# Attention weighing with 64-column products, row sums from ScalarE's accumulator, halves added on VectorE

## What is computed

```python
query, key, value = layernorm(x) @ w_q.T, ctx @ w_k.T, ctx @ w_v.T
scores = einsum('bghnd,bgsd->bghns', query, key) / 32 ** 0.5
scores = where(mask, scores, finfo.min)
attention = softmax(scores, axis=-1)
out = einsum('bghns,bgsd->bghnd', attention, value)
x = x + out.reshape(b, n, 1024) @ w_out.T
x12 = layernorm(x) @ w12.T + b12
x = x + (silu(x12[:1024]) * x12[1024:]) @ w3.T + b3
```

## Time and profile before

| what | value |
|---|---|
| median of 3 runs | 1041.52 us (1041.49 to 1042.86) |
| profiled execution, span | 1040.4 us |
| TensorE matmuls busy | 1017.7 us, 98% |
| TensorE weight loads busy | 695.6 us, 67% |
| VectorE busy | 661.6 us, 64% |
| ScalarE busy | 447.3 us, 43% |
| GpSimd busy | 498.6 us, 48% |

### The profile page before, as it was taken

The page is one execution under the profiler, slowest core; times in us unless marked ns, Lnnn a source line. Parts: engine busy times, 40 slices in busy tenths (PEclk is TensorE's granted clock), DMA queues, the critical chain, the costliest instruction groups (busy, mean ns, idle before and its releaser), DMA issues.

```text
span 1040.4 us, 21876 instructions
## 1 busy us (share of the span) xinstructions
PE 1017.7 (98%) x8400; PEld 695.6 (67%) x8400; DVE 661.6 (64%) x2080; ACT 447.3 (43%) x983; POOL 498.6 (48%) x476
## 2 busy tenths in 40 slices
PE   7897999999999999999999999999999999999998
PEld 6786868869687696886655544444444888468853
DVE  6789977767787777888646234636864447625431
ACT  6768556557465574664766210123431112202100
POOL 2869923727337273379958596158742301212000
PEclk9999999999999999999999999999999999999999
DMA  9669686998989999789946715494758631974201
GB/s 367 227 160 197 168 216 168 222 247 222 248 211 229 230 245 244 179 236 232 268 94 123 253 71 203 94 345 160 272 200 185 235 112 40 236 230 122 83 31 51
DMA packets 230776, 199.12 MB, mean 191 GB/s; under 512 B 177040, under 2 KB 187280, under 8 KB 225808
## 3 DMA queue, kind: packets, MB, share of 16 engines
q1 hardware_dynamic: 230672, 197.72, 69.0%
HBM read 119.04 MB, written 35.65 MB: 149 GB/s over the span
## 4 chain that ended last, share of the span: by engine, by line
PE 87%; DVE 6%; DMA 1%; ACT 1%; issue 0%; SPq 0%; DVEq 0%
PE bank_dense L1349 52%; PE bank_spare L1349 13%; PE bank_score L1494 6%; PE bank_spare L1494 6%; PE bank_av L1494 3%; PE bank_score L1406 2%; DVE arena_attn L1820 2%; DVE arena_attn L1830 1%; PE bank_av L1424 1%; PE bank_av L1428 1%; PE bank_av L1426 1%; PE bank_dense L1366 1%; DMA k_scratch<-arena_in 1%; PE bank_spare L1358 0%; PE bank_dense L1358 0%
## 5 line engine op out<-in xcount | busy, mean ns | idle before, releaser
L1153 ACT ACTIVATE arena_attn<-arena_attn,arena_in 128x128 f32<-128x128 f32 x512 | 162.7, 391 | 94.6 <-DVE arena_in L1820 93.6
L1349 PE MATMUL bank_dense<-arena_rows,arena_in 128*128 128x256 f16 (+1 forms) x1272 | 175.2, 295 | 1.9 <-POOL arena_in L874 1.0
L936 POOL TENSOR_TENSOR arena_attn<-arena_attn 128x512 f16<-128x512 f32 x89 | 102.6, 1170 | 148.8 <-ACT arena_attn L1160 148.8
L1349 PE MATMUL bank_dense<-arena_attn,arena_rows 128*128 128x512 f16 x768 | 166.4, 379 | 0.0
L1349 PEld LDWEIGHTS bank_dense<-arena_rows,arena_in 128*128 128x128 f16 x1272 | 123.0, 98 | 43.1 <-DVE arena_in L1668 1.6
L1820 DVE CUSTOM_DVE_ANT_0 arena_attn<-bank_score,arena_in 128x128 f32<-128x128 f32 x512 | 143.5, 346 | 0.4 <-PE bank_score L1406 0.4
L1349 PEld LDWEIGHTS bank_dense<-arena_attn,arena_rows 128*128 128x128 f16 x768 | 75.2, 98 | 90.2
L1349 PE MATMUL bank_dense<-arena_out,arena_attn 128*128 128x512 f16 x576 | 127.8, 379 | 0.0
L1349 PEld LDWEIGHTS bank_dense<-arena_out,arena_attn 128*128 128x128 f16 x576 | 55.5, 98 | 63.3
L1349 PE MATMUL bank_spare<-arena_rows,arena_in 128*128 128x256 f16 (+1 forms) x648 | 87.6, 292 | 0.0
L1349 PE MATMUL bank_dense<-arena_out,arena_in 128*128 128x512 f16 x384 | 83.0, 379 | 0.0
(11 more groups left out here) (219 smaller groups left out, 1890.8 us busy)
## 6 DMA issues: line engine op xcount, KB each, us to landing
arena_rows<-x SPq DMA_DIRECT2D x32, 512.0 KB, 6.1
arena_in<-w_scratch SPq DMA_DIRECT2D x64, 256.0 KB, 3.1
arena_attn<-q_scratch SPq DMA_DIRECT2D x48, 256.0 KB, 4.5
arena_rows<-w_t SPq DMA_DIRECT2D x12, 1024.0 KB, 6.2
arena_rows<-ctx_t SPq DMA_DIRECT2D x8, 1024.0 KB, 6.1
q_scratch<-arena_attn SPq DMA_DIRECT2D x16, 512.0 KB, 5.1
x_scratch<-arena_rows SPq DMA_DIRECT2D x16, 512.0 KB, 3.8
arena_out<-x_scratch SPq DMA_DIRECT2D x16, 512.0 KB, 5.9
```

The lines of the kernel that those rows point to most:

```text
L936: ins = pool.tensor_tensor(p_split[:, g % 2, u, 1], e[:, g % 2, u], p_split[:, g % 2, u, 0], ALU.subtract)
L1153: ins = act.activation(head, head, ACT.Exp, bias=neg_max[:, g % 2, h:h + 1], scale=-1.0)
L1349: ins = pe.matmul(dst, lhs(a, c), rhs(b, c), start=(c == chunks[0] and n == 0), stop=(c == chunks[-1] and n == 2))
```

## The change

From group 8 on (`PAIRED_FROM`), V is stored as high and low part side by side (`v_both`, 64 columns a group), and high P meets both in one product of 64 columns; low P meets the high part (32 columns). Two products a head stand where three stood. Groups 0 to 7 keep three products, of 32 columns. The column of ones is gone. The row sums come from the accumulator of ScalarE's exponentials (`accum_out` into `p_sum`) for all 64 groups. `divide` reads 8 x 64 results from group 8 on and writes them to `weighed`; `add_pairs` adds the two halves into `attn`, and `turn_attn` waits for that addition by a semaphore of its own.

```diff
-VW = DH + 1
+VW = 2 * DH
+PAIRED_FROM = 8
...
+        weighed = part(arena_attn, 59, 2, F32).rearrange("p (h w) -> p h w", w=VW)
+        p_sum = part(arena_attn, 61, 1, F32)[:, 0:4 * U * HPG].rearrange("p (r h) -> p r h", r=4)
...
-        v_high = sb("v_high", [P, 2, U, GROUPS, VW], F16)
-        v_low = sb("v_low", [P, 2, U, GROUPS, DH], F16)
+        v_both = sb("v_both", [P, 2, U, GROUPS, VW], F16)
...
-            pool.memset(v_high[:, :, :, :, DH:DH + 1], 1.0).then_inc(s_vinit, 1)
...
-                    ins = act.activation(head, head, ACT.Exp, bias=neg_max[:, g % 2, h:h + 1], scale=-1.0)
+                    ins = act.activation(head, head, ACT.Exp, bias=neg_max[:, g % 2, h:h + 1], scale=-1.0,
+                                         accum_out=p_sum[:, g % 4, h:h + 1])
...
             def turn_attn(g):
-                pe.wait_ge(s_avread, g + 1)
+                if g < PAIRED_FROM:
+                    pe.wait_ge(s_avread, g + 1)
+                else:
+                    pe.wait_ge(s_attn, g + 1 - PAIRED_FROM)
...
-                        pe.matmul(B_AV[:, at:at + VW], prob_t[:, g % 2, u, 0, j], v_high[:, a % 2, u, m],
-                                  start=True, stop=False)
-                        pe.matmul(B_AV[:, at:at + DH], prob_t[:, g % 2, u, 0, j], v_low[:, a % 2, u, m],
-                                  start=False, stop=False)
-                        ins = pe.matmul(B_AV[:, at:at + VW], prob_t[:, g % 2, u, 1, j], v_high[:, a % 2, u, m],
...
+                        else:
+                            pe.matmul(B_AV[:, at:at + VW], prob_t[:, g % 2, u, 0, j], v_both[:, a % 2, u, m],
+                                      start=True, stop=False)
+                        ins = pe.matmul(B_AV[:, at:at + DH], prob_t[:, g % 2, u, 1, j], v_both[:, a % 2, u, m, 0:DH],
                                         start=False, stop=True)
...
             def divide(g):
-                av = B_AV[:, 0:VW * U * HPG].rearrange("p (h w) -> p h w", w=VW)
+                av = B_AV[:, :].rearrange("p (h w) -> p h w", w=VW)
+                n = DH if g < PAIRED_FROM else VW
+                dst = attn.rearrange("p (h w) -> p h w", w=DH) if g < PAIRED_FROM else weighed
+                dve.wait_ge(s_exp, 2 * g + 2)
+                dve.reciprocal(inv_sum[:, :], p_sum[:, g % 4]).then_inc(s_inv, 1)
                 dve.wait_ge(s_av, g + 1)
...
+            def add_pairs(g):
+                if g >= PAIRED_FROM:
+                    dve.wait_ge(s_avread, g + 1)
+                    dve.tensor_tensor(attn.rearrange("p (h w) -> p h w", w=DH), weighed[:, :, 0:DH], weighed[:, :, DH:],
+                                      ALU.add).then_inc(s_attn, 1)
...
                     mask_scores(g)
+                    if g >= 3:
+                        add_pairs(g - 3)
```

More of the change, by code:

```diff
@@ L409, in xattn_ffn @@
         kept, with_6, with_5, with_7 = [terms[:, 0], terms[:, 1]], terms[:, 2], terms[:, 3], terms[:, 4]
+        weighed = part(arena_attn, 59, 2, F32).rearrange("p (h w) -> p h w", w=VW)
+        p_sum = part(arena_attn, 61, 1, F32)[:, 0:4 * U * HPG].rearrange("p (r h) -> p r h", r=4)
         k_stack = part(arena_attn, 63, 4).rearrange("p (b g n) -> p b g n", b=2, g=4)
         temp_late = part(arena_attn, 63, 2, F32)
-        v_high = sb("v_high", [P, 2, U, GROUPS, VW], F16)
-        v_low = sb("v_low", [P, 2, U, GROUPS, DH], F16)
+        v_both = sb("v_both", [P, 2, U, GROUPS, VW], F16)
         stage = [part(arena_attn, at, 2).rearrange("p (s n) -> p s n", s=2) for at in (56, 58, 60)]
-        stage.append(v_low.rearrange("p r u g w -> p (r u g w)").rearrange("p (s n) -> p s n", s=2))
-        stage.append(v_high.rearrange("p r u g w -> p (r u g w)")[:, 0:2 * HALF].rearrange("p (s n) -> p s n", s=2))
+        stage += [v_both.rearrange("p r u g w -> p (r u g w)")[:, 2 * HALF * n:2 * HALF * n + 2 * HALF]
+                  .rearrange("p (s n) -> p s n", s=2) for n in range(2)]
         q_in = [part(arena_attn, at, 8, F32) for at in (8, 16, 24, 32)]
@@ L1143, in v_hi @@
                 act.wait_ge(s_dense, done("v", t, u))
-                act.activation(v_high[:, t % 2, u, :, 0:DH],
+                act.activation(v_both[:, t % 2, u, :, 0:DH],
                                bank("v", t, u)[:, 0:KV].rearrange("p (g w) -> p g w", g=GROUPS), ACT.Copy,
@@ L1228, in _ @@
             o_sum(3)
-            act.wait_ge(s_vinit, 1)
             v_hi(0, 0)
@@ L1423, in weigh @@
                         at = VW * (HPG * u + j)
-                        pe.matmul(B_AV[:, at:at + VW], prob_t[:, g % 2, u, 0, j], v_high[:, a % 2, u, m],
-                                  start=True, stop=False)
-                        pe.matmul(B_AV[:, at:at + DH], prob_t[:, g % 2, u, 0, j], v_low[:, a % 2, u, m],
-                                  start=False, stop=False)
-                        ins = pe.matmul(B_AV[:, at:at + VW], prob_t[:, g % 2, u, 1, j], v_high[:, a % 2, u, m],
+                        if g < PAIRED_FROM:
+                            pe.matmul(B_AV[:, at:at + DH], prob_t[:, g % 2, u, 0, j], v_both[:, a % 2, u, m, 0:DH],
+                                      start=True, stop=False)
+                            pe.matmul(B_AV[:, at:at + DH], prob_t[:, g % 2, u, 0, j], v_both[:, a % 2, u, m, DH:],
+                                      start=False, stop=False)
+                        else:
+                            pe.matmul(B_AV[:, at:at + VW], prob_t[:, g % 2, u, 0, j], v_both[:, a % 2, u, m],
+                                      start=True, stop=False)
+                        ins = pe.matmul(B_AV[:, at:at + DH], prob_t[:, g % 2, u, 1, j], v_both[:, a % 2, u, m, 0:DH],
                                         start=False, stop=True)
@@ L1800, in v_lo @@
             def v_lo(t, u):
-                low(v_low[:, t % 2, u], bank("v", t, u)[:, 0:KV].rearrange("p (g w) -> p g w", g=GROUPS),
-                    KV_FACTOR, v_high[:, t % 2, u, :, 0:DH], ("v", t, u))
+                low(v_both[:, t % 2, u, :, DH:], bank("v", t, u)[:, 0:KV].rearrange("p (g w) -> p g w", g=GROUPS),
+                    KV_FACTOR, v_both[:, t % 2, u, :, 0:DH], ("v", t, u))
             def block_scales(a):
@@ L2037, in _ @@
                 divide(NG - 11 + s)
+                add_pairs(NG - 11 + s)
                 if s > 8:
```

10 lines of the change are left out of this document (5 added, 5 removed).

## The result

The changed kernel takes 1064.5 us (median of 4 runs, 1062.4 to 1067.4), the kernel before 1042.2 beside it: a ratio of 1.0205, 95% interval 1.0185 to 1.0225. The profiled execution after has a span of 1063.3 us, 22.9 more than the 1040.4 of before. The forecast of 1059 (1046 to 1070) had the sign right and missed 5 of the 22 us.

What follows compares the result with a forecast made beforehand. TensorE, busy 98% of the span, was taken as the bound. Terms of 18.0, 3.7, 0.5, 1.5 and -6.0 gave +17.7 us on 1040.4, so 1058.1, and 1059 us for the runs' median; range 1046 to 1070.

Steps and rivals of the forecast that it cites:

- TensorE is the bound, and a wait of it counts in full: Between 180 and 500 us TensorE is busy 319.94 of 320 us; every nanosecond it waits ends the kernel later.
- The weighing saves 0.17: On TensorE, a group's weighing takes 0.43 us, 0.17 less; over 56 groups at most 9.5 us.
- Division +0.26, addition 0.44: On VectorE, dividing 512 instead of 256 elements costs +0.26 us; the new addition of 256 takes 0.44 us.
- Waiting for GpSimd 0.35: In steps 0 to 2 the addition waits 0 to 0.69 us for GpSimd's instruction; half, 0.35, was taken.
- The upper bound of 0.69: The longest wait of the addition for a GpSimd instruction, 0.69 us.
- Rival C's upper form: The addition always waits the full 0.69 for GpSimd: 1064 us, or 1069 with 6.4 for block 1; 12%.
- Turning at T+4.82, T+5.01 in step 0: After weighing starts (T), turning waits for the addition: steps 0 to 2, blocks 3 to 7, 1.14 or 1.32 longer, +18.0 us.
- Gains kept in the covered steps, -6.0 and +0.5: 35 groups keep their 0.17 us, -6.0; step 3, late behind step 2, costs 0.5 in all.
- Step 7, +3.7: VectorE hands out later by 0.61 us, pushing back the second v product in 6 blocks: +3.7 us.
- Sums on ScalarE, +1.5: Accumulator reads add 0.8 us per group; only block 1 pays, +1.5 us, bounds 0 and 6.4.
- B: Accumulator reads put ScalarE on the path in most steps; at half of them +22 us, 1081; 5%.

Runs made afterwards that it cites:

- the run with one read in eight: Changed kernel with ScalarE's accumulator read for one head in eight only: 1065.4 us; likewise with addition first and one half in PSUM: 1041.8 us.
- the run with one half in PSUM: Changed kernel with the division split in two and the high half left in PSUM, so the addition has one SBUF source: 1059.7 us.
- the run with the sums alone: Kernel before with only accumulator output added to ScalarE's 512 exponentials, the sums unused: 1046.3 us, ratio 1.0022.
- the addition-first order: Changed kernel with the addition moved from behind the eight masked minima to directly behind the division: 1059.9 us.
- both edits together: Changed kernel with the addition directly behind the division and its high half left in PSUM: 1052.9 us, ratio 1.0097.
- the covered steps: Changed kernel with pairs only for groups whose turning stands behind a product of 512 columns, the others keeping three products: 1048.0 us.
- the kernel that also leaves step 7 alone: Seven of eight heads paired, sums on TensorE, one half in PSUM, addition first, old form in step 7 and block 7's steps 1, 2: 1038.0 us.
- the run with two additions: Changed kernel with a second addition of the same halves into an unused tile ahead of each real one: 1096.7 us, one run.

## Why the prediction was right, and where it was off

The steps in the prediction's order:

The forecast lies in its range, and the wait it named is the one that costs. But part of its nearness is luck, as said at the single steps.

1. **TensorE is the bound, and a wait of it counts in full.** Right, and once more than in full: 22.8 us between the first and the last weighing, 22.9 in the span, with 1.67 by the clock after a wait. The forecast had no term for the clock. It also added 1.1 us from span to run time by comparing two different executions; within one execution it is 2.1 for the kernel before (1042.3 and 1040.2) and 1.8 for the changed one (1065.1 and 1063.3).
2. **The weighing saves 0.17.** Right: 0.44 in the rows above, -0.17 in every step without a wait, in all runs with 64 columns.
3. **Division +0.26, addition 0.44.** 0.69 less 0.42 is 0.27; the addition alone takes 0.42. Right. VectorE's half rate for two float32 sources in SBUF, of which the Trainium skill warns for one form ("Vector Engine (DVE) Microarchitecture Reference", section "Points that are easy to get wrong"), does not show in this addition, which is another form: 422 ns with both sources in SBUF, 421 with one in PSUM.
4. **Waiting for GpSimd 0.35.** In blocks 3 to 6 the mean is 0.32: 0.11, 0.85 and 0.00 in steps 0, 1, 2. The mean was right by luck and the picture wrong. It is no chance meeting: these three values repeat in all four blocks, and in the run with one read in eight, so step 1 hits each time and step 2 never. The upper bound of 0.69 was too low as well; the longest addition, 1389 ns, waited 0.97. The rows agree with the rule in the Trainium skill ("SBUF — State Buffer", section "Who interferes with whom"), and the run with one half in PSUM shows that both sources have to be in SBUF for it. Rival C's upper form gave 1064, which is the time measured; its mechanism, the full wait each time, isn't what happened.
5. **Turning at T+4.82, T+5.01 in step 0.** Measured T+4.81 (step 0), T+5.36 (step 1), T+4.51 (step 2); a mean of 4.89 against a forecast of 4.88, which is luck again, since the single steps are off by -0.20, +0.54 and -0.31. In block 5 the three steps last 7.70, 8.25 and 7.40 us, where the forecast had about 7.6 and the kernel before 6.52, 6.51 and 6.53 (312.94 less 306.42 is 6.52, not 6.51). Block 7 is the term that was mis-sized: 3.6 forecast, 6.0 measured, of which 1.67 is the clock and 0.7 the lateness of VectorE. In its step 2 two tiles' row statistics (3.4 us) stand ahead of the division:

```profile
471.31 0.41 DVE L1800 SCALAR_TENSOR_TENSOR arena_attn<-bank_dense,arena_attn 128x256 f16<-128x256 f32 x1
471.64 0.15 DVE L1651 COPY small<-bank_spare 128x8 f32<-128x8 f32 x1
471.71 0.19 DVE L1848 RECIPROCAL arena_in<-arena_attn 128x8 f32<-128x8 f32 x1
472.01 0.69 DVE L1851 TENSOR_TENSOR arena_attn<-bank_av,arena_in 128x512 f32<-128x512 f32 x1
474.79 0.41 DVE L1858 TENSOR_TENSOR arena_in<-arena_attn 128x256 f32<-128x256 f32 x1
...
475.26 0.44 PE L1372 MATMUL bank_dense<-arena_in 128*128 128x128 f32 x2 [2.50 <-DVE arena_in L1858]
```

   T is 469.08, so the division is at T+2.9 and not T+1.2. Before, the same lateness was hidden: the division alone was done 0.6 before the turning. The rows of block 5 were taken to stand for all five blocks; they held for four.

6. **Gains kept in the covered steps, -6.0 and +0.5.** Measured -2.9 for -5.5. Of the gain 1.7 is lost in steps 5 and 6 of block 7, where the addition is issued at T+6.29 and T+5.88 (T+3.8 to T+4.5 in blocks 3 to 6) and the turning waits 0.95 and 0.34, and 0.5 in step 3 of block 2, where it waits 0.30. The margin of the covered steps was taken from block 5 alone.
7. **Step 7, +3.7.** 4.2. The mechanism was right: in block 4 the reading of the x tiles' banks starts at T+5.67 where it was T+5.05, and the second v product at T+6.39 where it was T+5.80. In blocks 5, 6 and 7 the turning waits 0.24 to 0.30 too.
8. **Sums on ScalarE, +1.5.** +0.5 net in the first 135 us, which is no more than two traces differ by, and the run with the sums alone has +2.0 in its span and 3.1 in its medians. Near in size, but largely in another place: 0.8 us per group costs at the ends of the blocks and not in steps 0 to 2. That it is hidden where ScalarE waits for VectorE, and costs where VectorE waits for ScalarE, fits this and wasn't tested by itself.

The four misses (+3.0 in the tight steps, 1.67 of it by the clock, +0.5 in step 7, +2.6 of lost gain, -1.0 in the first blocks) make the 5.1 us between forecast and measurement. Of the rivals, none held: B (ScalarE on the path) is refuted for the changed kernel by the run with one read in eight. In the addition-first order the same reads do cost 11 us.

**Three forecasts of experiments failed largely for one reason.** For the addition-first order, for both edits together and for the covered steps I asked only whether the turning still waits, and took it that without a wait the time comes back. VectorE's extra 0.8 us per group is paid at whatever it hands out next in order: the minima, the q low halves, the scales and x banks of step 7, and the weight tile whose load is gated by a maximum. The run with one read in eight, one source in PSUM and the addition first came back to the time of before (1041.8), and the kernel that also leaves step 7 alone went below it.

## What to carry to other kernels

A product saved on TensorE is paid by whoever combines its result: here 0.17 us saved against 0.7 to 1.6 us more on VectorE, in a path that had 2 us of slack in most steps and less in a few. Write down the slack of every kind of step, the rare ones too, before counting gains, and count what is handed out behind the new instruction as well as its direct reader. An edit's price depends on the order it stands in: the accumulator reads cost nothing in one order and 11 us in the other, so test an edit in the version that will be kept. And look at the granted clock in short stretches: an average of 0.99 over 320 us hid 1.67 us in one product.

## What the runs showed of the hardware that was not expected

- An addition of 256 float32 with both sources in SBUF took 415 to 1389 ns beside a busy GpSimd; with one source in PSUM 415 to 427. The wait falls at fixed places and is not random.
- The next product starts 29 ns after one of 64 float16 columns, as had been worked out, and 25 ns after one of 32, so the second 32 columns cost 4 ns.
- TensorE's granted clock fell to 0.50 for a while after some waits of 2.3 to 2.7 us and not after others of the same length: three of four in step 1 of the run with two additions. Where the same step can be compared with and without the fall, it was 1.6 to 1.7 us longer.
- Reading ScalarE's accumulator is its own instruction (189 ns in the row, 0.10 us until the next one starts). Four exponentials, from the start of the first to the copy behind them, take 1.56 us with reads (263.18 to 264.74, addition first and one half in PSUM) and 1.18 without (258.69 to 259.87, one read in eight), so eight cost about 0.8:

```profile
L1156 ACT ACTIVATION_READ_ACCUMULATOR arena_attn<-arena_attn,arena_in 128x1 f32 x512 | 96.7, 189 | 0.0
```
